# A product that nothing reads behind each hop of a triangular solve

## The chip, the cores and the metric

The kernel runs on one core of a Trainium2 chip. Its time is the device time of one execution in microseconds (us); lower is better. Three executions of the kernel before took 1478.14, 1480.52 and 1487.08 us, median 1480.52.

## The reference

The model has four layers, each with a residual sum behind a layer norm: a selective scan, an attention with a mixture of experts, a causal layer, and the attention with experts again. The change lies in the causal layer, for 4 batches of 512 positions, 16 heads of 8:

```python
probs = jax.nn.softmax(logits + causal_mask, axis=-1)
L = jnp.eye(s, dtype=probs.dtype) - jnp.tril(probs, -1)
rhs = jnp.diagonal(probs, axis1=-2, axis2=-1)[..., None] * v
A = jax.scipy.linalg.solve_triangular(L, rhs, lower=True)
```

So every position is the weighted sum of all earlier solved positions and its own value, and the solve is serial along the positions.

## The kernel before

The function `delta_phase` computes this layer. It works on 16 tiles of 128 positions, four to a batch; the loop index is `n`, and `t = n % 4` is the tile's place in its batch. Each engine has a program written out by hand in the same order: a loop over `n` from -6 to 15, and inside it 14 numbered places, the hooks `h` (0 to 13). At a hook `beside(n, h)` puts in work for later tiles: row maxima of tile `n + 4` or `n + 3` (L2772 and L2775 on TensorE, read by VectorE at L2559), scores of tile `n + 3` (L2790, L2793, L2802, read by ScalarE at L2400 and L2405), the sums of tile `n + 2`, and at hooks 9 to 12 the products `mt` of tile `n + 1` (L2839, copied by ScalarE at L2412). Between these stands the solve of tile `n` itself.

The solve of a tile: for `t` above 0 the earlier tiles' contribution (L2887), turned (L2906); then a product with the inverses of the 16x16 diagonal blocks (L2915, at hook 2); then seven hops (L2928), at hooks 3, 5, 7, 9, 10, 11 and 12. Before each hop VectorE transposes 32 columns of the step's PSUM bank into `a_hop` (L2700), and behind the last one ScalarE copies the solved tile to `aT` (L2452). A hop is 16 small fp32 products, each with 16 or 32 rows and 32 columns of the array, four of them side by side on the diagonal of the array. The last of them raises the semaphore `at_ps` for VectorE or ScalarE. Then TensorE goes on with the next hook.

Transfers are queued on SyncE: the sums of a tile go to DRAM and back (`z_scr`), GpSimd inverts the blocks, and the inverses go out and back (`x_scr`) before `mt` can be computed. The keys and queries of the next batch (`k_scr`, `q_scr`) are loaded once the last scores of the batch before have been computed.

PSUM has eight banks of 512 fp32 columns per partition: two for the steps, `TURN` (number 2) for two transposes a tile, two that ScalarE reads and three that VectorE reads. `TURN` is written at the start of a tile (`turned`, L2938, and `turn_right_side`, L2906) and read by ScalarE (L2456) and VectorE (L2691) before the product of L2915.

`mask_diag4` is a bf16 table of 128x512 and `ident_b` the bf16 identity; `score` uses the same pair at L2790 to start a bank.

Of the kernel before, what the change touches and what calls it, by code (L numbers as in the profile page):

```python
# [1918 lines left out]
def delta_phase(core, nc):  # L1919

    x_sb, w = core.x, core.w
    q_scr, k_scr, m_scr = core.q_scr, core.k_scr, core.md_scr
    e_scr, z_scr, x_scr = core.e_scr, core.z_scr, core.x_scr
    with ExitStack() as ctx:
# [3 lines left out]
        ps = ctx.enter_context(nc.psum_tensor("d_ps", [P, 8, 512], F32))  # L1928

        STEP, TURN, TO_ACT, TO_DVE = (0, 1), 2, (3, 4), (5, 6, 7)  # L1930
# [252 lines left out]
        def all_mt(n):  # L2183
            return in_act("mt", n, len(MT_HOOKS) - 1)
# [8 lines left out]
        with nc.Block() as block:  # L2193
# [525 lines left out]
            def _(pe):  # L2719
# [5 lines left out]
                def dve_free(kind, n, i=0):  # L2725
                    if dve_place[kind, n, i] >= 3:
                        pe.wait_ge(s["dve_out"], dve_place[kind, n, i] - 2)
                    return dve_bank(kind, n, i)
# [115 lines left out]
                def beside(n, h):  # L2844
                    if n >= 1 and h == 0:
                        output(n - 1)
                    m = later_tile_at(turned_sums_at, n, h)
                    if m is not None:
                        turn_sums(m)
                    if starts_in(n, 4) is not None and h in (6, 7):  # L2850
                        own_scores(starts_in(n, 4), h - 6)
                    m = maxima_done(n, h)
                    if m is not None:
                        turn_maxima(m)
                    for i in scores_in(n, h):
                        score(n + 3, i)
                    for m, hd in maxima_in(n, h):
                        for_maximum(m, hd)
                    if in_program(n + 1) and h in MT_HOOKS:
                        multiplied(n + 1, MT_HOOKS.index(h))  # L2860
                    m = later_tile_at(sums_at, n, h)
                    if m is not None:
                        sums(m)
                    m = tile_at(column_at, n, h)
                    if m is not None:
                        turn_column(m)
                    if goes_on(n, LEAD) is not None and h == 12:
                        turn_in(goes_on(n, LEAD))
                    if batch_at(values_at, n, h) is not None:
                        project_values(batch_at(values_at, n, h))  # L2870
                    if begins_early(n + 1) and h == 13:
                        first_tiles(n + 1)
                    if goes_on(n, 5) is not None and h in (0, 1):
                        project(goes_on(n, 5), h)

                def output(n):
                    pe.wait_ge(s["at_sb"], n + 1)
                    nc.tensor.matmul(dve_free("output", n)[:, 0:P], aT[:, n % 2, :], w["d_wd"], start=True, stop=True).then_inc(
                        s["dve_ps"], 1)
# [17 lines left out]
                def from_earlier(n):  # L2897
                    t = n % TPB
                    pe.wait_ge(s["an_sb"], turned_tiles(n - 1))
                    if n >= 2:  # L2900
                        pe.wait_ge(s["at_sb"], n - 1)
                    earlier_tiles(n, range(t - 1, t)).then_inc(s["g_ps"], 1)

                def turn_right_side(n):
                    pe.wait_ge(s["gT_sb"], later_tiles(n))
                    nc.tensor.transpose(ps[:, TURN, 0:P], gT[:, :], core.ident[:, :]).then_inc(s["gn_ps"], 1)  # L2906

                def inverse(n):
                    pe.wait_ge(s["gn_sb"], n + 1)
                    if n >= 2:  # L2910
                        pe.wait_ge(s["at_sb"], n - 1)
                    for g in range(GROUPS):
                        for q in range(GROUP):
                            hd = g * GROUP + q
                            last = nc.tensor.matmul(ps[q * SPAN:(q + 1) * SPAN, STEP[n % 2], 0:P], of_head(g_pad[:, :], hd),  # L2915
                                                    xT[:, n % 2, hd, :], start=(g == 0), stop=(g == GROUPS - 1))
                    last.then_inc(s["at_ps"], 1)

                def hop(n, k):
                    if k == 1:  # L2920
                        pe.wait_ge(s["act_out"], all_mt(n))
                    pe.wait_ge(s["hop_in"], HOPS * n + k)
                    r = (k - 1) // 2
                    rows, cols = (BLK, slice(BLK, SPAN)) if k % 2 else (SPAN, slice(SPAN, P - r * SPAN))
                    for g in range(GROUPS):
                        for q in range(GROUP):
                            own = slice(q * SPAN, q * SPAN + rows)
                            last = nc.tensor.matmul(  # L2928
                                ps[q * SPAN:(q + 1) * SPAN, STEP[n % 2], r * SPAN + cols.start:r * SPAN + cols.stop],
                                a_hop[own, g * SPAN:(g + 1) * SPAN],  # L2930
                                mT[own, n % 2, g, SPAN_AT[r] + cols.start:SPAN_AT[r] + cols.stop],
                                start=False, stop=(g == GROUPS - 1), skip_group_check=True)
                    last.then_inc(s["at_ps"], 1)

                def turned(n):
                    pe.wait_ge(s["at_sb"], n + 1)
                    pe.wait_ge(s["gn_sb"], n + 1)
                    nc.tensor.transpose(ps[:, TURN, 0:P], aT[:, n % 2, :], core.ident[:, :]).then_inc(s["an_ps"], 1)  # L2938

                for n in range(-LEAD, TILES_N):  # L2940
                    later = n >= 0 and n % TPB
                    if n == 0:
                        pe.wait_ge(s["set"], 4)
                        pe.wait_ge(s["zero_set"], 2)
                    if later:
                        turned(n - 1)
                    for h in range(HOOKS):
                        beside(n, h)
                        if later and h == 0:
                            from_earlier(n)  # L2950
                        if later and h == 1:
                            turn_right_side(n)
                        if n >= 0 and h == 2:
                            inverse(n)
                        if n >= 0 and h in HOP_AFTER:
                            hop(n, HOP_AFTER[h])
                output(TILES_N - 1)

# [86 lines left out]
```

## Time and profile before

| | |
|---|---|
| median of 3 runs | 1480.52 us |
| the profiled execution, its own time | 1479.21 us |
| its span, first to last instruction | 1477.3 us |
| TensorE (PE) busy | 1156.5 us, 78% |
| VectorE (DVE) busy | 999.9 us, 68% |
| ScalarE (ACT) busy | 684.1 us |
| GpSimd (POOL) busy | 631.6 us |
| granted clock of TensorE, mean | 0.868 |

### The profile page before, as it was taken

Reading aid. Unit: us, or ns where it says so; the run is one execution under the profiler, and the core shown is the slowest. Engines: PE = TensorE matmul, PEld = TensorE weight load, DVE = VectorE, ACT = ScalarE, POOL = GpSimd, SP = SyncE. Lnnn points to the kernel's source line nnn. Section 1 sums busy time; section 2 is a strip of 40 time slices with the busy share of each in tenths; the row PEclk is TensorE's granted clock in tenths of the full one; section 3 lists DMA queues with packets and bytes.
Section 4 is the critical chain, followed back from the end, with each engine's and each line's share of the span. In section 5 each row is a group of like instructions: output and inputs, shape, how many; then the busy total and the mean of one; then the engine's idle time right before and its main releaser. Section 6 shows DMA issues by size and latency. Waiting matters only on the chain. (4 is left out here: it accounts for less than half of the span.)

```text
span 1477.3 us, 32913 instructions
## 1 busy us (share of the span) xinstructions
PE 1156.5 (78%) x12859; PEld 628.3 (43%) x12890; DVE 999.9 (68%) x2098; ACT 684.1 (46%) x1380; POOL 631.6 (43%) x838
## 2 busy tenths in 40 slices
PE   6746776869999998636868877968866699999976
PEld 2212232323333327623546655645655333333276
DVE  6699999978898965446635635625621688989653
ACT  3833334406667674512603513432341066676754
POOL 2279979852435124413334324422432524351244
PEclk9878879879999998856868968977997599999998
DMA  5388834033133121262241141141120331331213
GB/s 168 140 278 311 300 142 146 32 82 88 27 97 93 44 79 49 65 130 34 37 87 22 30 103 19 23 105 27 20 53 11 68 88 35 88 94 42 83 48 91
DMA packets 137744, 128.49 MB, mean 87 GB/s; under 512 B 92007, under 2 KB 123559, under 8 KB 132202
## 3 DMA queue, kind: packets, MB, share of 16 engines
q1 hardware_dynamic: 129536, 118.50, 29.1%
q0 software_dynamic: 2496, 5.13, 1.1%
q10 hardware_dynamic: 5558, 2.76, 0.9%
q8 instruction: 102, 1.67, 0.5%
q14 instruction: 52, 0.43, 0.1%
HBM read 105.55 MB, written 38.62 MB: 98 GB/s over the span
## 5 line engine op out<-in xcount | busy, mean ns | idle before, releaser
L1391 DVE TENSOR_REDUCE f_row_min<-f_ps 128x1 f32<-128x512 f32 x512 | 323.8, 676 | 55.1 <-PE f_ps L1718 54.8
L1281 ACT ACTIVATE f_e<-f_ps 128x512 f32<-128x512 f32 x512 | 283.0, 602 | 125.0 <-PE f_ps L1738 123.2
L1718 PE MATMUL f_ps<-f_operands 72*128 72x512 bf16 x512 | 204.6, 409 | 27.7 <-DMA f_operands<-k_scr 16.2
L1738 PE MATMUL f_ps<-f_operands 75*128 75x512 bf16 x512 | 189.5, 380 | 2.6 <-ACT f_e L1281 2.6
L788 PE MATMUL m_ps<-m_shared,sb_ident 128*128 128x512 f32 x256 | 136.1, 681 | 58.2 <-DVE m_shared L628 58.1
L361 POOL TENSOR_TENSOR m_drive<-m_du,m_ring 128x1024 f32<-128x1024 f32 x64 | 149.6, 2351 | 56.2 <-DVE m_ps L620 37.7
L2559 DVE TENSOR_REDUCE d_row_min<-d_ps 128x1 f32<-128x384 f32 (+3 forms) x176 | 104.6, 630 | 74.3 <-PE d_ps L2775 73.6
L493 ACT ACTIVATE m_ps<-m_delta,m_A 128x511 f32<-128x511 f32 x128 | 83.0, 681 | 131.6 <-DVE m_ps L620 109.0
L1749 PE MATMUL f_ps<-f_e,f_v_op 128*32 128x512 f32 x1024 | 136.4, 604 | 2.1 <-ACT f_e L1281 1.4
L1718 PEld LDWEIGHTS f_ps<-f_operands 72*128 72x128 bf16 x512 | 51.2, 100 | 180.6 <-DVE f_row_min L1391 129.2
L788 PEld LDWEIGHTS m_ps<-m_shared,sb_ident 128*128 128x128 f32 x256 | 52.6, 216 | 143.7 <-DVE m_shared L628 86.9
L620 DVE TENSOR_TENSOR_SCAN m_ps<-m_ps,m_drive 128x1024 f32<-128x1024 f32 x44 | 101.1, 2297 | 4.9
L2212 POOL TENSOR_TENSOR d_xT_blk<-d_e_blk,d_zi_blk 128x256 f32<-128x256 f32 x16 | 13.3, 832 | 202.9 <-DVE d_zi_blk L2620 202.9
L2772 PE MATMUL d_ps<-d_k_op,d_q_op 96*128 96x128 bf16 (+3 forms) x256 | 71.4, 360 | 36.1 <-DMA d_k_op<-k_scr 23.0
L2412 ACT COPY d_mT<-d_ps 128x320 f32<-128x320 f32 x64 | 27.3, 426 | 131.0 <-PE d_ps L2839 130.2
L2839 PE MATMUL d_ps<-d_xT,d_e_nat 128*32 128x128 f32 (+3 forms) x2048 | 64.1, 282 | 24.6 <-DMA d_xT<-x_scr 21.9
L2928 PE MATMUL d_ps<-d_mT,d_a_hop 16*32 16x16 f32 (+3 forms) x3584 | 71.3, 216 | 8.0 <-DVE d_a_hop L2700 7.0
L2223 POOL TENSOR_TENSOR d_xT_blk<-d_xT_blk,d_prod 128x14 f32<-128x14 f32 (+6 forms) x224 | 63.8, 285 | 17.5
L2700 DVE STREAM_TRANSPOSE d_a_hop<-d_ps 128x32 f32<-128x32 f32 x112 | 23.7, 211 | 70.0 <-PE d_ps L2928 57.5
L1168 POOL DMA_INDIRECT y_scr<-f_operands x46 | 53.7, 1168 | 38.8 <-DVE f_operands L1607 36.9
L2839 PEld LDWEIGHTS d_ps<-d_xT,d_e_nat 128*32 128x32 f32 x2048 | 55.5, 135 | 34.8 <-DMA d_xT<-x_scr 23.8
L2218 POOL TENSOR_TENSOR d_prod<-d_xT_blk 128x14 f32<-128x14 f32 (+6 forms) x224 | 62.1, 277 | 17.5
(295 smaller groups left out, 2177.2 us busy)
## 6 DMA issues: line engine op xcount, KB each, us to landing
m_ring<-bc_scr SPq DMA_DIRECT2D x32, 1024.0 KB, 5.4
f_rows_scr<-blank SPq DMA_DIRECT2D x2, 8707.5 KB, 31.1
f_wall<-f_wall SPq DMA_DIRECT2D x16, 578.0 KB
f_operands<-q_scr SPq DMA_DIRECT2D x32, 288.0 KB
f_operands<-k_scr SPq DMA_DIRECT2D x96, 96.0 KB
d_q_op<-q_scr SPq DMA_DIRECT2D x6, 576.0 KB
d_k_op<-k_scr SPq DMA_DIRECT2D x18, 192.0 KB
f_operands<-f_rows_scr SPq DMA_DIRECT2D x46, 64.5 KB, 1.8
```

Of the source, the lines that this page charges most:

```text
L361: nc.gpsimd.tensor_tensor(drive[:, step % AHEAD, :].rearrange("p (a s) -> p a s", a=HALVES), du[:, :, tokens(b)], b_row(step).unsqueeze(1) ...
L493: last = nc.scalar.activation(ps[:, at + 1:at + S], delta[:, k, b * S + 1:(b + 1) * S], ACT.Exp, scale=A[:, k, n:n + 1])
L620: nc.vector.tensor_tensor_scan(h, bank(DECAY + HALVES * (step % 2), HALVES), drive[:, step % AHEAD, :], 0.0, ALU.mult, ALU.add).then_inc(s ...
L788: last = nc.tensor.matmul(bank(Y + k), core.ident[:, :], hC[:, k * S:(k + 1) * S], start=False, stop=last_of_batch)
L1281: nc.scalar.activation(e_sb[:, n % 3, hh, :], ps[:, SCORE[(b * UNITS + u) % SCORE_BANKS], :], ACT.Exp, scale=SCALE).then_inc(s["e_out"], 1)
L1391: nc.vector.tensor_reduce(row_min[:, b % 2, u // TPB, u % TPB:u % TPB + 1], ps[:, MAXQ[(b * UNITS + u) % MAX_BANKS], :], AX.X, ALU.max, ne ...
L1718: nc.tensor.matmul(ps[:, MAXQ[n % MAX_BANKS], :], q_op(b, QK)[:, hd, t * P:(t + 1) * P], k_op(b, QK)[:, hd, :], start=True, stop=True).the ...
L1738: nc.tensor.matmul(ps[:, SCORE[n % SCORE_BANKS], :], k_op(b, QKS)[:, hd, t * P:(t + 1) * P], q_op(b, QKS)[:, hd, :], start=True, stop=True ...
L1749: last = nc.tensor.matmul(ps[hh * HEAD_COLS:(hh + 1) * HEAD_COLS, O_BANK, :], v_of(b, t, g * GROUP + hh), e_sb[:, n % 3, hh, :], start=(t ...
L2559: nc.vector.tensor_reduce(row_min[:, n % 2, g * heads:(g + 1) * heads], dve_bank("maximum", n, g)[:, 0:heads * cols].rearrange("p (h c) -> ...
L2772: nc.tensor.matmul(bank[:, hh * cols:(hh + 1) * cols], q_op[0:SHIFT_AT, hd, rows_of(t)], k_op[0:SHIFT_AT, hd, 0:cols], start=(hh == 0), st ...
L2839: last = nc.tensor.matmul(bank[q * SPAN:(q + 1) * SPAN, SPAN_AT[r]:SPAN_AT[r] + P - first], e_nat[:, n % 3, hd, first:first + SPAN], xT[:, ...
```

## The change

Behind each of the seven hops of each tile TensorE computes one more product: the identity, over all 128 rows and columns of the array, with the 512 columns of `mask_diag4`, bf16, into the bank `TURN`. It raises no semaphore and waits for none. Nothing reads the result; the next product that uses the bank starts it anew.

```diff
@@ -2932,6 +2932,9 @@
                                 start=False, stop=(g == GROUPS - 1), skip_group_check=True)
                     last.then_inc(s["at_ps"], 1)
 
+                def keep_busy():
+                    nc.tensor.matmul(ps[:, TURN, :], w["ident_b"], w["mask_diag4"], start=True, stop=True)
+
                 def turned(n):
                     pe.wait_ge(s["at_sb"], n + 1)
                     pe.wait_ge(s["gn_sb"], n + 1)
@@ -2954,6 +2957,7 @@
                             inverse(n)
                         if n >= 0 and h in HOP_AFTER:
                             hop(n, HOP_AFTER[h])
+                            keep_busy()
                 output(TILES_N - 1)
```

The order of the other instructions stays as it is on every engine; only PE's program grows, by 16 x 7 = 112 products. The difference of PE's program at the first two hops of tile 0 (L2928 is the hop, L2936 the added product, L2802 scores and L2755 sums for later tiles):

```order
 L2828 MATMUL d_ps<-sb_ident,d_z_col 16x128
 L2928 MATMUL d_ps<-d_mT,d_a_hop 32x16 x16
+L2936 MATMUL d_ps<-sb_mask_diag,sb_ident_b 128x512
 L2802 MATMUL d_ps<-d_q_op,d_k_op 128x128 x12
 L2928 MATMUL d_ps<-d_mT,d_a_hop 32x96 x16
+L2936 MATMUL d_ps<-sb_mask_diag,sb_ident_b 128x512
 L2755 MATMUL d_ps<-sb_head_sum,d_swap 128x16 x2
 L2802 MATMUL d_ps<-d_q_op,d_k_op 128x128 x6
```

The added product stands between the hop and the work for later tiles; the hop's semaphore is raised ahead of it.

## Rows read from the trace of the kernel before

**Rows 1.** The page: span, busy time of engines, granted clock in 40 slices.
```profile
span 1477.3 us, 32913 instructions
...
PE 1156.5 (78%) x12859; PEld 628.3 (43%) x12890; DVE 999.9 (68%) x2098; ACT 684.1 (46%) x1380; POOL 631.6 (43%) x838
...
PEclk9878879879999998856868968977997599999998
```

**Rows 2.** Windows by tile: us; PE, PEld, DVE, ACT, POOL busy; PEclk; DMA share; GB/s.
```profile
723.70:756.00 32.30, 23.05 (x594) 17.49 (x592) 10.48 (x25) 13.64 (x33) 11.33 (x33) 0.86 0.51 110
756.00:788.10 32.10, 24.17 (x518) 17.74 (x524) 16.26 (x43) 6.03 (x15) 9.64 (x31) 0.66 0.20 28
788.10:818.60 30.50, 25.70 (x607) 18.87 (x608) 17.31 (x53) 10.22 (x22) 12.00 (x33) 0.89 0.20 33
818.60:841.20 22.60, 19.42 (x528) 14.39 (x529) 17.95 (x45) 9.13 (x20) 11.14 (x30) 0.92 0.12 13
841.20:871.70 30.50, 24.27 (x594) 18.98 (x592) 10.26 (x26) 13.58 (x33) 10.27 (x32) 0.80 0.50 113
871.70:904.20 32.50, 23.52 (x518) 17.44 (x524) 16.27 (x44) 6.03 (x15) 9.63 (x31) 0.71 0.20 31
904.20:937.20 33.00, 27.59 (x607) 20.56 (x608) 17.15 (x54) 10.32 (x22) 12.00 (x33) 0.84 0.20 32
937.20:957.90 20.70, 18.55 (x535) 13.68 (x536) 17.83 (x45) 9.16 (x21) 9.56 (x27) 1.00 0.07 9
1023.70:1054.80 31.10, 24.89 (x599) 18.18 (x601) 16.52 (x53) 10.41 (x22) 10.79 (x32) 0.89 0.18 30
1099.70:1151.20 51.50, 31.88 (x1161) 26.27 (x1160) 5.82 (x26) 5.47 (x16) 9.66 (x31) 0.76 0.09 14
723.70:1151.20 427.50, 327.32 (x8461) 246.97 (x8486) 193.37 (x531) 136.09 (x319) 147.45 (x441) 0.82 0.24 46
```

**Rows 3.** What PE waited for in 723.7:1151.2: total us, times, longest.
```profile
PE d_ps L2772 <- DMA d_k_op<-k_scr: 23.0, 6, 6.3
PE d_ps L2839 <- DMA d_xT<-x_scr: 21.9, 9, 7.3
PE d_ps L2780 <- DVE d_row_min L2559: 20.5, 9, 4.3
PE d_ps L2928 <- DVE d_a_hop L2700: 7.0, 19, 0.6
```

**Rows 4.** The tile d_ps: the hop's products, min/median/max ns, forms.
```profile
L2928 PE MATMUL d_ps<-d_mT,d_a_hop x3584: 171/209/365, 725.1 to 1150.6; 16*32 16x16 f32 x116, 32*32 32x96 f32 x28, 32*32 32x64 f32 x28, 32*32 32x32 f32 x28
```

**Rows 5.** Timeline of PE, one 512-column product at the higher clock level.
```profile
787.99 0.39 PE L2790 MATMUL d_ps<-sb_mask_diag,sb_ident_b 128*128 128x512 bf16 x1
788.21 0.27 PE L2793 MATMUL d_ps<-d_k_op,d_q_op 128*128 128x128 bf16 x2
```

**Rows 6.** Timeline of PE, one 512-column product at the lower clock level.
```profile
752.18 0.63 PE L2775 MATMUL d_ps<-sb_mask_up,sb_ident_b 128*128 128x512 bf16 x1
752.60 0.42 PE L2906 MATMUL d_ps<-sb_ident,d_gT 128*128 128x128 f32 x1
```

**Rows 7.** Timeline of PE: four idle gaps behind hops, with what ended them.
```profile
742.26 0.33 PE L2938 MATMUL d_ps<-sb_ident,d_aT 128*128 128x128 f32 x1 [0.40 <-ACT d_aT L2452]
...
798.00 1.03 PE L2839 MATMUL d_ps<-d_xT,d_e_nat 128*32 128x128 f32 x32 [2.58 <-DMA d_xT<-x_scr]
...
987.85 0.61 PE L2772 MATMUL d_ps<-d_k_op,d_q_op 96*128 96x128 bf16 x4 [6.26 <-DMA d_k_op<-k_scr]
...
1007.62 0.38 PE L2780 MATMUL d_ps<-sb_ident,d_row_min 128*16 128x128 f32 x1 [2.90 <-DVE d_row_min L2559]
```

**Rows 8.** Timeline of PE and DVE, one round of the last tile.
```profile
1148.28 0.62 PE L2928 MATMUL d_ps<-d_mT,d_a_hop 16*32 16x16 f32 x32 [0.34 <-DVE d_a_hop L2700]
1148.97 0.22 DVE L2700 STREAM_TRANSPOSE d_a_hop<-d_ps 128x32 f32<-128x32 f32 x1 [0.74 <-PE d_ps L2928]
```

**Rows 9.** Window inside the tile that starts at 756.0, no long gap.
```profile
759.00:768.90 9.90, 9.88 (x132) 6.48 (x132) 7.21 (x18) 0.47 (x2) 0.00 (x0) 0.50 0.25 42
```

## The prediction, made before the changed kernel ran

> **What bounds the kernel now.** I read the page first: PE is busy for 1156.5 of 1477.3 us, and its granted clock is high nearly everywhere except at the start and in the middle [rows 1]. The change touches only the solves, so I then read windows by tile. The sixteen solves take 427.5 us, with PE busy for 327.3 and DVE for 193.4, at a clock of 0.82 [rows 2]: PE works at its lower level for 2 x 0.18 x 427.5 = 154 us. Third, the waits: the 100 us in which PE is idle there are in good part waits for transfers, 23.0 us for keys and 21.9 us for block inverses, and 20.5 us for DVE's row maxima; the hops themselves waited only 7.0 us for DVE's transposes [rows 3]. So PE sets the pace between a few waits that others set, and both a longer PE program and a faster PE clock show only in part.
>
> **The added work, gross.** The nearest row is the same product with the same operands, L2790: from its start to the next product's start 788.21 - 787.99 = 0.22 us at the higher level [rows 5]. At the lower level a product of the same size took 752.60 - 752.18 = 0.42 us [rows 6]. With 36% of the time at the lower level the mean is 0.64 x 0.22 + 0.36 x 0.42 = 0.29 us, and 112 of them are 32.7 us. That is the upper end of the cost, with nothing hidden. The trace has no product of this kind between two packed groups; I take the price as it is, since the hop's small products (171 to 365 ns each, four side by side) [rows 4] give way to full-array products in the same program already.
>
> **What of it is hidden.** A product behind a hop costs nothing if PE would have waited before the next thing that matters, and the wait's end doesn't depend on it. I go by the tile's place t in its batch; seven products each, 1.5 us at the higher level, up to 2.9 at the lower.
> - t = 0. Hops 1 to 3 stand ahead of the wait for inverses (2.58 us in one case [rows 7]), whose chain started a tile earlier; I count them hidden for most of it. Hops 4 to 7 stand ahead of the wait for the next batch's keys (6.26 us [rows 7]), whose loads were released by earlier scores. The seventh also falls into the 0.40 us in which PE waits for ScalarE's copy [rows 7]. Left over: about 0.6 us a tile, 4 tiles, 2.4 us.
> - t = 1. Hops 1 to 3 lie in the row maxima that DVE limits, with a wait of 2.90 us at their end [rows 7] against 3 x 0.42 = 1.3 us added. Hops 4 to 7 stand before small waits for ScalarE. Left: 0.6 us, 4 tiles, 2.4 us.
> - t = 2. Hops 1 to 4 are ahead of waits for inverses and maxima, 5 to 7 are exposed. Left: 0.8 us, 4 tiles, 3.2 us.
> - t = 3. PE is densest here, 18.55 of 20.70 us [rows 2]; small waits for maxima and copies take up most. Left: 0.4 us, 3 tiles, 1.2 us.
> - The last tile has nothing beside the hops. From the end of the hop (1148.28 + 0.62 = 1148.90) DVE's transpose starts at 1148.97 and takes 0.22 us, and PE idles 0.34 us before the next hop [rows 8]. The product streams through most of that gap. I count 0.1 us in all.
>
> The sum is 9.3 us. The transfers are not delayed much: what releases them is later by the same few tenths. If these covers go (a transfer released late by the products, a faster load), up to the full 32.7 us shows; the lower end is 0.
>
> **What it may give back: the clock.** Tiles of the same kind at different clocks tell what the lower level costs. For t = 3: 22.60 us at 0.92 against 20.70 us at 1.00, so 2 x 0.08 x 22.6 = 3.6 us at the lower level cost 1.9 us. For t = 2: 33.00 us at 0.84 (10.6 us low) against 31.10 at 0.89 (6.8 us low), 1.9 us for 3.8 us more [rows 2]; the third, 30.50 us at 0.89, lies beside the second. So with t = 2 and 3 about 0.55 us is lost for each us at the lower level. With t = 0 and 1 there is no such relation: 32.30 us at 0.86 against 30.50 at 0.80, and 32.10 at 0.66 against 32.50 at 0.71 [rows 2]; their waits for transfers take up the difference.
>
> How much low time goes cannot be read from a row; it is bounded by none and by all. In rows 9 PE is busy for 9.88 of 9.90 us and the clock stays at 0.50 throughout [rows 9]. So being busy was not enough there; what runs in it are products over 96 rows and hops that use 16 or 32 rows and columns each [rows 4]. The added product uses the whole array, which most of the beside work does not, and the clock may rise for it. The Trainium skill, page "TensorE: Matmul & The Clock Gate", section "What's actually happening", says that the gate is set by how busy PE has been recently and that activity releases it; taken as busy time it would have the clock high in this window, which the trace contradicts, and it would give the added products nothing to do there.
>
> I take half of the low time for t = 2 and 3 in the first three batches. There it is 6.7 + 3.6 + 10.6 + 0 + 6.8 = 27.7 us over the five rows, so 13.9 x 0.55 = 7.6 us. From 1099.7 on, where PE is only 62% busy, 0.48 x 51.5 = 24.7 us are low [rows 2]; a third of that at 0.4 gives 3.3 us. The rest of the low time, some 102 us with t = 0 and 1, I count at nothing, since waits stand behind it. Together 11 us. The bounds: nothing, and all of it, 0.55 x 27.7 + 0.5 x 24.7 + 0.15 x 102 = 43 us.
>
> **The sum** is 1479.2 + 9.3 - 11 = 1477.5 us for an execution like the profiled one, which lies 1.3 us under the median of the three. Against the median: **1479 us**. Under 1% (15 us, so 1465.7 to 1495.3) counts as no change that can be told.
>
> **The rivals.**
> - *The clock doesn't move.* By the skill's rule read as busy time. The mechanism here: where the clock is low, PE waits around the hop, or is busy already as in rows 9. Then only the 9.3 us remain: 1490 us. For it, rows 9; against it, that the product uses four to eight times as much of the array as four small products of a hop side by side [rows 4]. 15%, no change.
> - *The products lie on the path (slower).* Place: between a hop and the beside work at hooks 3 to 12. ScalarE and DVE get scores, maxima and `mt` later by 0.22 to 0.42 us each, and SP sends sums and inverses later, so that the waits for transfers move instead of shrinking. Two thirds unhidden are 22 us: 1502 us with the clock as it is; all of it 1513. It decides from 15 / 32.7 = 46% unhidden with no clock returned. For it: PE is the busiest engine in every tile [rows 2]. Against: some 65 us of waits for transfers and maxima [rows 3] stand behind the hops. 18%.
> - *The clock stays high through most of it (faster).* Two thirds of the bound on the gain, 29 us, less 9: 1460 us. It decides when over 24 us are given back. For it: seven products a tile are spread over the tile, also where the clock falls. Against: in the long waits, 6.26 us and the like [rows 7], no hop stands. 20%.
> - *It doesn't do what it says*: `TURN` would have to be in use or the product to bring a wait. Program order shows neither. 2%, 1480 us.
>
> The forecast itself has 45%.
>
> **Range and chances.** Within 1%: 45 + 15 + 2 = 62%; faster 20%; slower 18%. The range takes in half of either side case: from 1462 to 1499 us.
>
> **What would show it.** In the changed trace, the line of the added product: 112 of them, starts 0.22 us or 0.42 us ahead of the next product. The clock over the solves above 0.82, with the tiles of t = 3 at 1.00 near 21 us, and those of t = 2 above 0.89. The wait of PE for DVE's row maxima and for the inverses shorter by about a third. The tiles with t = 0 and 1 within 1 us of before. The forecast is wrong if the clock over the solves stays at 0.82 and the waits don't shrink (slower), or if it goes over 0.92 (faster).

## The result and the profile after

In 20 executions each, the changed kernel took 1487.25 us (median; 1481.16 to 1495.94) and the kernel before 1481.29 us (1476.72 to 1489.74). The ratio is 1.0036, with a 95% interval of 1.0019 to 1.0054: 5.3 us slower (2.8 to 8.0). It lies within the 1% that the forecast counted as no change and in its range, but the forecast of 1479 us was on the other side of 1, and the loss is clear of noise. One execution of either kernel is a few us off its median, so a cost of 5 us is read from the timed ratios; the profiles, one execution each (1486.8 us here), tell where clock and waits moved.

The page of the changed kernel, the lines that answer to [rows 1]:

```profile
span 1485.0 us, 33058 instructions
...
PE 1155.3 (78%) x12892; PEld 632.8 (43%) x13002; DVE 999.6 (67%) x2098; ACT 683.7 (46%) x1380; POOL 630.9 (42%) x838
...
PEclk9879889869999998857969977978987699999988
```

The windows by tile, in the columns of [rows 2] and at the same places of the program (tile by tile from the step's first transpose, then the tail and all solves):

```profile
722.40:755.80 33.40, 23.33 (x595) 18.32 (x601) 9.97 (x26) 13.57 (x33) 11.56 (x34) 0.86 0.50 106
755.80:788.80 33.00, 24.14 (x523) 17.72 (x531) 16.16 (x44) 6.02 (x15) 9.57 (x31) 0.73 0.19 28
788.80:820.40 31.60, 26.09 (x609) 19.53 (x615) 17.66 (x54) 10.21 (x22) 11.97 (x33) 0.89 0.21 33
820.40:842.10 21.70, 18.99 (x534) 14.41 (x541) 17.63 (x44) 9.11 (x20) 10.02 (x29) 1.00 0.10 12
842.10:874.80 32.70, 22.69 (x591) 17.92 (x594) 10.39 (x27) 13.57 (x33) 11.54 (x34) 0.86 0.48 108
874.80:907.40 32.60, 23.42 (x523) 17.38 (x531) 16.05 (x43) 6.02 (x15) 9.57 (x31) 0.77 0.19 28
907.40:939.80 32.40, 27.04 (x609) 20.37 (x616) 17.64 (x53) 10.22 (x22) 11.97 (x33) 0.84 0.21 32
939.80:961.30 21.50, 19.04 (x537) 14.42 (x544) 17.86 (x45) 9.21 (x21) 9.84 (x28) 1.00 0.10 12
1027.40:1057.90 30.50, 26.09 (x601) 19.54 (x607) 16.67 (x53) 10.39 (x22) 10.73 (x32) 0.83 0.19 31
1106.00:1159.20 53.20, 32.18 (x1167) 26.70 (x1182) 5.94 (x26) 5.46 (x16) 9.57 (x31) 0.81 0.08 13
722.40:1159.20 436.80, 327.76 (x8495) 251.50 (x8601) 193.28 (x531) 135.86 (x319) 147.43 (x442) 0.85 0.24 45
```

The solves take 436.8 us where they took 427.5 [rows 2]. The clock over them rose from 0.82 to 0.85, so 2 x 0.15 x 436.8 = 131 us are low instead of 154. The tiles show where. The tile with t = 3 that was at 0.92 is at 1.00 and takes 21.70 instead of 22.60 us; the one that was at 1.00 before takes 21.50 instead of 20.70, so seven products, 1.5 us gross, cost 0.8 us there. The forecast had 0.4. The tiles with t = 2, where the forecast looked for the return, stand at 0.89, 0.84 and 0.83, no better than 0.89, 0.84 and 0.89 before [rows 2]. Those with t = 1 rose, from 0.66 and 0.71 to 0.73 and 0.77, and did not get shorter (33.00 and 32.60 us). Those with t = 0 take 33.40 and 32.70 us, 1.1 and 2.2 us longer. The tail went from 0.76 to 0.81, 24.7 to 20.2 us low, and takes 53.20 us instead of 51.50.

What PE waited for in the solves, as [rows 3] (total us, times, longest):

```profile
PE d_ps L2839 <- DMA d_xT<-x_scr: 25.2, 9, 7.2
PE d_ps L2772 <- DMA d_k_op<-k_scr: 23.4, 6, 5.3
PE d_ps L2780 <- DVE d_row_min L2559: 17.3, 12, 3.7
```

Two of these waits were to shrink by a third. The one for the row maxima shrank from 20.5 to 17.3 us, the one for the inverses grew from 21.9 to 25.2 [rows 3]. The trace has every weight load of the new products, but not every product (kind, count, min/median/max ns, first and last start):

```profile
L2936 PEld LDWEIGHTS d_ps<-sb_mask_diag,sb_ident_b x112: 94/96/103, 724.3 to 1158.7; 128*128 128x128 bf16 x112
L2936 PE MATMUL d_ps<-sb_mask_diag,sb_ident_b x18: 389/390/607, 726.9 to 1157.9; 128*128 128x512 bf16 x18
```

So 94 products are missing in its PE busy time, and the idle time of this profile is overstated; the profile of the narrow products below has all 112. The price is as forecast, as one product at the higher level shows in the timeline, 822.46 - 822.23 = 0.23 us:

```profile
822.23 0.39 PE L2936 MATMUL d_ps<-sb_mask_diag,sb_ident_b 128*128 128x512 bf16 x1
822.46 0.61 PE L2802 MATMUL d_ps<-d_q_op,d_k_op 128*128 128x128 bf16 x8
```

### The profile page after: what moved, and what is told of

Same layout as the page of the kernel before. It is cut to its first block and busy times, and to the rows that moved or that the text cites. A ratio compares the mean times of both kernels' runs of the same rounds, so it can differ in the third digit from the quotient of the medians.

```text
span 1485.0 us, 33058 instructions
## 1 busy us (share of the span) xinstructions
PE 1155.3 (78%) x12892; PEld 632.8 (43%) x13002; DVE 999.6 (67%) x2098; ACT 683.7 (46%) x1380; POOL 630.9 (42%) x838
## 5 line engine op out<-in xcount | busy, mean ns | idle before, releaser
L2212 POOL TENSOR_TENSOR d_xT_blk<-d_e_blk,d_zi_blk 128x256 f32<-128x256 f32 x16 | 13.3, 833 | 206.6 <-DVE d_zi_blk L2620 206.6
L2772 PE MATMUL d_ps<-d_k_op,d_q_op 96*128 96x128 bf16 (+3 forms) x256 | 68.9, 351 | 37.1 <-DMA d_k_op<-k_scr 23.4
L2839 PE MATMUL d_ps<-d_xT,d_e_nat 128*32 128x96 f32 (+3 forms) x2048 | 63.7, 279 | 36.1 <-DMA d_xT<-x_scr 25.2
L2928 PE MATMUL d_ps<-d_mT,d_a_hop 16*32 16x16 f32 (+3 forms) x3584 | 69.1, 213 | 3.5 <-DVE d_a_hop L2700 2.8
```

The costliest lines, as they stand in the source:

```text
L2839: last = nc.tensor.matmul(bank[q * SPAN:(q + 1) * SPAN, SPAN_AT[r]:SPAN_AT[r] + P - first], e_nat[:, n % 3, hd, first:first + SPAN], xT[:, ...
```

## The experiments

All ratios are against the kernel before on the same chip, with 95% intervals. Each kernel ran 12 times, e11_full_rows 11 and e10_narrow_double 6 times. Two terms were open, the hidden share of the products and the return of the clock.

**e1_narrow** takes the array away and leaves the stream:

```diff
-                    nc.tensor.matmul(ps[:, TURN, :], w["ident_b"], w["mask_diag4"], start=True, stop=True)
+                    nc.tensor.matmul(ps[0:32, TURN, :], w["ident_b"][0:32, 0:32], w["mask_diag4"][0:32, :], start=True, stop=True)
```

> The added product keeps its 512 columns and its place, but uses 32 rows and 32 columns of the array instead of 128 and 128, so PE streams as long as in the changed kernel. Theory A (the clock did give back about 10 us as forecast, and the hidden part was overrated, so that some 15 us of the products lie on the path): without the return the time is the kernel before plus 14 to 17 us, ratio about 1.010, and the clock over the solves is back at about 0.82. Theory B (the products cost the 6 us that are seen, and the clock returns nothing): the same as the changed kernel, ratio about 1.004. The low time in the solves (152 us before, 133 us changed) tells too: A wants it at 150 or more.

Measured: 1490.21 us, ratio 1.0068 (1.0041 to 1.0096), 10 us slower. Its window over the solves and its waits:

```profile
721.90:1159.40 437.50, 359.85 (x8573) 254.26 (x8598) 193.24 (x530) 136.07 (x319) 147.93 (x442) 0.81 0.24 45
```

```profile
PE d_ps L2839 <- DMA d_xT<-x_scr: 19.2, 9, 5.0
PE d_ps L2780 <- DVE d_row_min L2559: 16.8, 9, 3.8
PE d_ps L2772 <- DMA d_k_op<-k_scr: 15.6, 5, 4.9
```

The clock is at 0.81. At 0.38 x 0.42 + 0.62 x 0.22 = 0.30 us a product, 112 are 33 us gross. PE is busy for 359.85 us, 32.5 us more than before, while the solves grew by 437.5 - 427.5 = 10.0 us; so some 23 us went into idle time, which fell from 100.2 to 77.6 us. The three waits show 13.8 us of it: 15.6, 19.2 and 16.8 against 23.0, 21.9 and 20.5 [rows 3]. So a stream without the return costs 10 us, between the two theories (14 to 17, and 6). That is an upper bound for the cost term, forecast as 9.3, because the narrow products also leave the clock somewhat lower than it was before, as the clocks of all executions show below.

**e10_narrow_double** and **e3_double** put two narrow and two whole products behind each hop. The edit of e3 (e10 has the narrow line twice):

```diff
                     nc.tensor.matmul(ps[:, TURN, :], w["ident_b"], w["mask_diag4"], start=True, stop=True)
+                    nc.tensor.matmul(ps[:, TURN, :], w["ident_b"], w["mask_diag4"], start=True, stop=True)
```

> Two such products behind each hop instead of one. Theory A: the cost doubles to 30 us or a little more, since the gaps are used up, and the clock returns somewhat more than with one, 12 to 16 us: the kernel before plus 16 to 20 us, ratio about 1.012. Theory B: two times 6 us and what no longer fits in the gaps, 14 to 20 us, ratio 1.010 to 1.013. If the clock stays high almost throughout (over 0.92 in the solves), the time may come out under that of one product: ratio under 1.004.

> Two products behind each hop, each over 32 rows and 32 columns of the array, 512 columns long: the stream of e3_double without its use of the array. Theory A (the cost on the path is some 10 us for one product a hop, and the clock gave back 4 us of it with one whole-array product and much more with two): 20 to 24 us slower than before, ratio 1.014 to 1.016, against 1.0042 for e3_double. Theory B (the clock returns nothing, and a second product fits into gaps that the first has opened): the same as e3_double, 1.004.

Measured: the whole ones 1488.11 us, ratio 1.0042 (1.0018 to 1.0067); the narrow ones 1507.99 us, ratio 1.0198 (1.0171 to 1.0225). The same streams at the same places are 29 us slower or 6 us slower than the kernel before, by what part of the array they use. The whole ones came near the case that was set apart in their expectation (a clock over 0.92, a ratio under 1.004), the narrow ones lie above the 1.014 to 1.016 of theory A. The windows over the solves, the narrow ones first:

```profile
721.10:1171.60 450.50, 386.99 (x8685) 258.03 (x8710) 192.33 (x531) 136.52 (x319) 148.66 (x446) 0.81 0.23 43
```

```profile
719.20:1152.10 432.90, 338.50 (x8603) 243.89 (x8710) 193.00 (x531) 135.71 (x319) 148.43 (x446) 0.92 0.24 45
```

The clock is at 0.81 with the narrow products and at 0.92 with the whole ones. So, between two kernels with equal streams, the clock is worth about 23 us, and which of the two has the higher clock goes with the use of the array and not with busy time: PE is busy for 86% of the solves in the narrow kernel, and for 78% in the other, 83% if the 97 products that its trace lacks are added at 0.22 us. Part of the 23 us is the products' own price. In the narrow kernel, two of them start 0.22 us apart at the higher level and 0.43 at the lower:

```profile
725.52 0.37 PE L2936 MATMUL d_ps<-sb_mask_diag,sb_ident_b 32*32 32x512 bf16 x1
725.74 0.37 PE L2937 MATMUL d_ps<-sb_mask_diag,sb_ident_b 32*32 32x512 bf16 x1
...
734.90 0.63 PE L2936 MATMUL d_ps<-sb_mask_diag,sb_ident_b 32*32 32x512 bf16 x1
735.33 0.63 PE L2937 MATMUL d_ps<-sb_mask_diag,sb_ident_b 32*32 32x512 bf16 x1
```

With 38% and 16% of the solves low, 224 products are 224 x (0.38 - 0.16) x 0.2 = 10 us cheaper in e3_double.

**e11_full_rows** has all rows and 32 columns of the array:

```diff
-                    nc.tensor.matmul(ps[:, TURN, :], w["ident_b"], w["mask_diag4"], start=True, stop=True)
+                    nc.tensor.matmul(ps[0:32, TURN, :], w["ident_b"][:, 0:32], w["mask_diag4"], start=True, stop=True)
```

> One product behind each hop over all 128 rows but only 32 columns of the array, 512 long: PE streams as long as in the changed kernel, with a quarter of the array. Theory A (the return needs the whole array): like e1_narrow, 9 to 11 us slower than before, ratio 1.006 to 1.007. If what counts is that all rows are fed, it is like the changed kernel, 1.0036. Theory B (no return at all, e1_narrow's difference is chance): 1.0036 too; e10_narrow_double then tells these two apart.

Measured: 1487.17 us, ratio 1.0047 (1.0027 to 1.0067). The time tells nothing apart; for single products the intervals of whole, narrow and this one touch or overlap. The clock does. Over the solves it is at 0.86, with all 112 products in the trace, as high as in the changed kernel (0.85) and not as with the narrow ones (0.81):

```profile
724.10:1158.20 434.10, 348.67 (x8573) 249.21 (x8598) 194.28 (x531) 135.76 (x319) 147.89 (x441) 0.86 0.24 45
```

**The clock of every execution.** A profile is one execution, but every execution has its mean granted clock c over the whole program. With the span T, 2 x (1 - c) x T of it are at the lower level. Means over all executions:

| kernel | clock | kernel before | low time against before, us | time against before, by the ratio, us |
|---|---|---|---|---|
| changed | 0.880 | 0.872 to 0.874 | -17 to -23 | +5.3 |
| e1_narrow | 0.867 | 0.872 | +18 | +10.1 |
| e11_full_rows | 0.882 | 0.874 | -22 | +7.0 |
| e3_double | 0.896 | 0.872 | -70 | +6.2 |
| e10_narrow_double | 0.857 | 0.874 | +57 | +29.3 |
| e2_short | 0.871 | 0.872 | +3 | -1.2 |
| e4_late_tiles | 0.874 | 0.872 | -6 | +4.4 |
| e5_early_tiles | 0.879 | 0.873 | -16 | +5.6 |
| e7_t2_double | 0.878 | 0.873 | -13 | +3.1 |
| e6_fill_keys | 0.880 | 0.873 | -22 | -2.7 |
| e9_fill_both | 0.891 | 0.874 | -51 | -3.1 |
| e12_fill_more | 0.896 | 0.873 | -66 | -3.4 |

(For the changed kernel the clocks of its own runs of the kernel before are not on record; the range is that of the four chips of the experiments. The low times are good to about 10 us, that of e10 to about 20.)

Three things follow. First, 32 columns over all 128 rows raised the clock as much as the whole array did, and 32 columns over 32 rows lowered it: the single executions of e11_full_rows lie at 0.877 to 0.886, those of e1_narrow at 0.857 to 0.876. The rows made the difference, the other 96 columns none that shows. Second, the narrow products are no clean measure of the cost, since they add low time; the return against the kernel before is smaller than what separates whole from narrow. Third, the price of low time: between e10_narrow_double and e3_double 127 us of it go with 23 us, 0.18 us for each, with what the products themselves cost more at the lower level included. Between executions of one and the same kernel it is alike: in 109 of the kernel before, each us more at the lower level went with 0.20 us more time (correlation 0.66). That is a correlation, not an experiment, but the forecast had taken 0.5.

**e2_short** leaves whole-array products of 16 columns:

```diff
-                    nc.tensor.matmul(ps[:, TURN, :], w["ident_b"], w["mask_diag4"], start=True, stop=True)
+                    nc.tensor.matmul(ps[:, TURN, 0:16], w["ident_b"], w["mask_diag4"][:, 0:16], start=True, stop=True)
```

> The added product uses the whole array but streams 16 columns instead of 512: the weight load and the switch from small packed products to a whole-array product stay, the stream goes. Theory A and B both price the stream, so this should cost 112 x about 0.03 us = 3 us gross, 1 to 2 us on the path: ratio 1.000 to 1.001. Theory C (the switch itself costs, by breaking up the packed products): most of the 6 us stay, ratio 1.003 to 1.004.

Measured: 1481.18 us, ratio 0.9992 (0.9971 to 1.0013). Loading the identity and switching between packed and whole-array products costs nothing that can be measured (at most 2 us by the interval), and the clock stays where it was; the stream is the cost.

**Where the products stand.** e4_late_tiles keeps them for t = 2 and 3, e5_early_tiles for t = 0 and 1, e7_t2_double two of them for t = 2 only, e8_last_hop one only behind the seventh hop. The edit of e4; the others have `n % TPB < 2`, `n % TPB == 2` and `HOP_AFTER[h] == HOPS` as condition:

```diff
                             hop(n, HOP_AFTER[h])
+                            if n % TPB >= 2:
-                            keep_busy()
+                                keep_busy()
```

> The products stand only in the tiles with t = 2 and 3 (56 of 112), where the forecast placed the whole return of the clock. Theory A with the return where it was forecast: cost and return about cancel, ratio 0.999 to 1.001, and the loss of the changed kernel lies in the tiles with t = 0 and 1. Theory B: half of the loss, ratio 1.002. If it is 1.004 the loss lies in these dense tiles.

> The products stand only in the tiles with t = 0 and 1 (56 of 112), the other half of e4_late_tiles. If the losses of the two halves add up to that of the changed kernel (ratio 1.0036), this one has about 1.001, since e4 has 1.003. Theory A (a cost of about 9 to 10 us that the narrow product showed, less a return of the clock of about 4): these tiles hide the products behind the waits for keys and inverses as the forecast said, and the cost lies in t = 2 and 3. Theory D (the waits for transfers move with the products and hide nothing): ratio 1.003 here as well, and the halves don't add up because the clock's return in e4 is lost.

> Two products behind each hop, but only in the four tiles with t = 2 (56 products). In the profile of e3_double these tiles had 10 us at the lower level instead of 34, and took 112.3 instead of 117.2 us. Theory A (low time costs about half of itself in these tiles, as the forecast took it): 3 to 5 us faster than before, ratio 0.997 to 0.998. Theory B (the clock returns next to nothing): 3 to 6 us slower, ratio 1.002 to 1.004.

> A product only behind the seventh hop of each tile (16 products), where PE waits 0.35 to 0.40 us for ScalarE's copy of the solved tile, except ahead of the tiles with t = 2 and 3. Hidden as forecast: gross 4 us, about 1 us on the path, ratio 1.000 to 1.001. If that gap doesn't hide it, ratio 1.002 to 1.003.

Measured: e4 1.003 (1.0006 to 1.0053), e5 1.0038 (1.0021 to 1.0054), e7 1.0021 (0.9996 to 1.0046), e8 1.0001 (0.9979 to 1.0023). The halves cost 4.4 and 5.6 us, together 10 us, as much as the narrow products in all places, while the whole costs 5.3: it looks as if half of the products return next to nothing, though the intervals leave room for additive halves, and the low times do add up (6 and 16 us against 17 to 23). The tiles with t = 0 and 1 hide the products no better than the others; e5 leaves out the 1.001 of theory A. e7 missed: with two products the low time of the t = 2 tiles should have been worth more than the products, and it isn't, so the 0.55 us for each low us that I read from pairs of tiles doesn't arrive at the end. Its profile, which is its fastest execution (1476.86 us), has the three tiles with t = 2 of the first three batches:

```profile
787.10:816.20 29.10, 26.78 (x623) 18.17 (x622) 17.65 (x53) 10.23 (x22) 11.98 (x33) 1.00 0.21 34
903.20:933.20 30.00, 28.08 (x623) 18.97 (x623) 18.12 (x53) 10.22 (x22) 11.98 (x33) 0.94 0.21 33
1017.50:1048.30 30.80, 27.11 (x615) 17.92 (x614) 16.60 (x52) 10.40 (x22) 10.76 (x32) 0.94 0.19 32
```

Together they take 89.9 us, with 42 products in them, instead of 94.6 [rows 2], and are low for 7 us instead of 24. So in these tiles the return did come, about as the forecast priced it. 0.55 x 17 us given back, less 0.8 us for each of six sets of seven products, is 4.6 us. But the tiles with t = 0 of the same batches, which have no added product, take 101.7 us instead of 97.0 (36.2, 33.3 and 32.2 against 32.3, 30.5 and 34.2), and all solves 426.9 instead of 427.5. The gain is gone in the next tiles; with one execution each, whether by the transfers that they wait for or by chance stays open. Behind the seventh hop no cost of the products shows, as forecast, though the interval reaches to 3.4 us.

**Filling waits instead.** e6_fill_keys has no product behind a hop, but 12 and 8 ahead of the two waits for the keys of the next batch; e9_fill_both has also 4, 14 and 20 ahead of the wait for the inverses; e12_fill_more has 20 and 12, and 7, 24 and 32. In `for_maximum` and in `multiplied` (e9):

```diff
                     if n >= TPB and t == 0 and g * heads in (0, NH // 2):
+                        for _ in range(12 if g == 0 else 8):
+                            nc.tensor.matmul(ps[:, TURN, :], w["ident_b"], w["mask_diag4"], start=True, stop=True)
...
+                    if i == 0 and n >= 1:
+                        for _ in range({14: 14, 15: 20}.get(n, 4 if n % 2 else 0)):
+                            nc.tensor.matmul(ps[:, TURN, :], w["ident_b"], w["mask_diag4"], start=True, stop=True)
```

> No product behind a hop. Instead 12 and 8 such products ahead of PE's two waits for the next batch's keys (three batches, 60 products), where PE idles 2.3 to 6.3 us, so the products should be free (60 x 0.22 = 13 us, all inside 23.0 us of waits). Theory A: the clock enters the tiles with t = 1 at its higher level, their low time falls from 72 us to 30 to 45 us. If low time costs nothing there, as the forecast had it, ratio 0.999 to 1.001; if it costs 0.3 us for each us there, 10 us are gained, ratio 0.993 to 0.996. If the waits aren't free, ratio over 1.003.

> No product behind a hop. The 60 products ahead of the waits for keys as in e6_fill_keys, and 62 more ahead of PE's wait for the block inverses at hook 9: 4 in each of the tiles 0, 2, 4 to 12 where it waits 0.5 to 2.6 us, 14 and 20 in tiles 13 and 14, where it waits 4.9 and 7.3 us. If filling idle time is free and the clock enters the dense ends of the t = 2 tiles and the tail at its higher level, as I now hold: 3 us faster than e6_fill_keys, 5 to 6 us faster than before, ratio 0.996. If waits shorter than the filling make it late: ratio 0.999 to 1.001.

> As e9_fill_both with longer fillings: 20 and 12 products ahead of the two waits for keys (96 in all), 7 in each of seven tiles and 24 and 32 in tiles 13 and 14 ahead of the wait for inverses (105 in all). In e9_fill_both PE still waited 10.5 and 15.3 us at these two places. If low time is worth something where it is left, and filling stays free: 1 to 3 us faster than e9_fill_both, ratio 0.996 to 0.997. If, as I now hold, the low time that goes lies behind waits and row maxima and is worth next to nothing, while the longer fillings overrun some of the waits: ratio 0.998 to 1.001.

Measured: e6 1477.56 us, ratio 0.9982 (0.9961 to 1.0003); e9 1476.84 us, 0.9979 (0.9961 to 0.9996); e12 1479.91 us, 0.9977 (0.9956 to 0.9999). All three lie between what their two theories gave. For e6 and e9 no cost shows, and the kernels with 122 and 201 of them are about 3 us faster than the kernel before, with intervals that only just stay under 1; the kernel of this case is slower than both. The windows over the solves of e6, e9 and e12:

```profile
726.50:1148.40 421.90, 333.10 (x8549) 243.65 (x8547) 192.97 (x531) 136.09 (x319) 147.68 (x444) 0.87 0.25 46
```

```profile
720.80:1148.00 427.20, 336.48 (x8568) 244.79 (x8608) 193.73 (x531) 136.32 (x319) 150.70 (x447) 0.89 0.25 46
```

```profile
724.70:1155.20 430.50, 347.63 (x8647) 246.42 (x8687) 191.80 (x531) 135.99 (x319) 147.53 (x442) 0.91 0.25 45
```

The clock goes to 0.87, 0.89 and 0.91, so in these profiles 110, 94 and 77 us are low instead of 154 (over all executions the fall is smaller, 22, 51 and 66 us), and the gain stays at 3 us: the low time that went was worth next to nothing, or the fillings cost what it was worth. The latter isn't ruled out for e12, where PE waits for the inverses 0.4 us in all instead of 21.9, so that its longer fillings ran past some transfers. In return PE's wait for VectorE's row maxima grew from 20.5 us [rows 3] to 21.9, 27.6 and 30.9 us. The timeline of e6 in a tile with t = 1 shows how (in its numbering L2769 is the filling, L2774 and L2782 are L2772 and L2780 of before):

```profile
991.86 2.71 PE L2769 MATMUL d_ps<-sb_mask_diag,sb_ident_b 128*128 128x512 bf16 x8
994.40 0.39 PE L2774 MATMUL d_ps<-d_k_op,d_q_op 96*128 96x128 bf16 x4
...
996.39 0.28 PE L2782 MATMUL d_ps<-sb_ident,d_row_min 128*16 128x128 f32 x1 [0.46 <-DVE d_row_min L2559]
...
1006.59 0.38 PE L2782 MATMUL d_ps<-sb_ident,d_row_min 128*16 128x128 f32 x1 [4.63 <-DVE d_row_min L2559]
```

From 994.40 on PE is at the higher level (its products are 0.39 us long, not 0.61 to 0.64), is done with its part of the maxima sooner, and then waits 4.63 us for VectorE's last one, where it waited 2.90 us before [rows 7]. That product starts at 1006.59, 12.2 us behind the end of the wait for keys; before it started at 1007.62, 13.3 us behind it, with the clock at the lower level all the while. About 12 us at the higher level brought 1.1 us:

```profile
994.34 0.61 PE L2772 MATMUL d_ps<-d_k_op,d_q_op 96*128 96x128 bf16 x4 [2.31 <-DMA d_k_op<-k_scr]
```

## Why the prediction was wrong

- *Price of a product*, 0.22 and 0.42 us: right; 0.23 us in the changed kernel, 0.22 and 0.43 in e10_narrow_double. The doubt about packed groups is answered by e2_short: no cost of switching.
- *What is on the path*, 9.3 of 32.7 us: near in size, as far as the runs tell. Without any return it would be the 5.3 us measured, and e1_narrow gives at most 10 us (6 to 14) of 33. Its split over tiles isn't confirmed: e5_early_tiles costs at least as much as e4_late_tiles, where the forecast had 4.8 and 4.4 us with about 11 us of return in the latter. For t = 3 the tiles that were at 1.00 before and after show 0.8 us where the forecast had 0.4.
- *"I take half of the low time for t = 2 and 3"*, with a third for the tail, priced at 0.55 and 0.4: this is the step that failed, the return of 11 us. That the clock can give time back is shown by the doubled pair. Its size is at most 10.1 - 5.3 = 4.8 us for one product a hop (0 to 10 by the two intervals), since the narrow products add low time of their own. The amount of low time that went was as assumed (154 to 131 us in the profiles, 17 to 23 us over all executions, against 13.9 + 8.2), but not its place: the five rows of t = 2 and 3 hold 7.0 + 0 + 10.4 + 0 + 10.4 = 27.8 us of low time, against 27.7 before. It went with t = 1, from 21.8 to 17.8 and from 18.9 to 15.0 us in the two tiles shown, where the forecast rightly counted it at nothing, and in the tail, 4.5 us, which came out longer all the same. At the 0.18 to 0.20 us for each low us of all executions, some 20 us give 4 us: an estimate that agrees with 4.8.
- *The 0.55 us for each low us*: borne out inside the tiles with t = 2 of e7_t2_double, not at the end of the program. A tile that is shorter in the profile is not yet a shorter kernel; where e7's gain went stays open.
- *The reading of rows 9*, that products over 96 rows and small hops ran there: incomplete. Ten products of L2775 over the whole array ran there too, 4.23 us of PE's busy time, two of them 512 columns long, and the clock stayed at 0.50. So whole-array products don't bring the clock up everywhere, and the reason given for a rise was weaker than it looked:

```profile
759.32 0.63 PE L2775 MATMUL d_ps<-sb_mask_up,sb_ident_b 128*128 128x512 bf16 x1
```

- *Net*: -1.7 us forecast, +5.3 measured; 9.3 - 11 against at most 10.1 - 4.8. That it ended within 1% is luck, and no merit of the working: the cost and the return are both small against the 15 us.
- *The rival that the clock doesn't move* (1490 us) came near in time, but not in its mechanism: the clock over the solves rose from 0.82 to 0.85. The Trainium skill, page "TensorE: Matmul & The Clock Gate", section "What's actually happening", says that the gate is set by how busy PE has been recently. Read as busy time, this disagrees with the pair: PE is busy for 86% of the solves at 0.81 in e10_narrow_double, and for no more in e3_double at 0.92.
- *The rival on the path* (1502 us): its place was right for at most 10 us, not for 22.
- *The rival that the clock stays high* (faster) needs two products a hop, and then they cost more than the clock returns: e3_double, 0.92 and yet 1.0042.
- *What would show it*: waits for maxima and inverses a third shorter was wrong, they went from 20.5 to 17.3 and from 21.9 to 25.2 us; t = 2 above 0.89 was wrong, and so was t = 0 within 1 us (1.1 and 2.2 us longer); a clock above 0.82, t = 1 within 1 us and t = 3 at 1.00 near 21 us were right.

## What to carry to other kernels

Before one adds work to hold TensorE's clock, take the same stream with a corner of the array and with all its rows; the pair shows what the clock is worth, and one kernel alone does not. The corner gives only an upper bound on the cost, because it can lower the clock: look at the granted clock of all executions, not at one profile. Low time is worth something only where PE's own stream ends last; ahead of a wait for a transfer or for VectorE it was worth next to nothing here, however much of it there was. Such work belongs ahead of a wait that is longer than it, where it did no harm, rather than behind each step of a serial chain; even there it brought only 3 us of 1480.

## What the runs showed of the hardware

- With equal streams at equal places, two products a hop over 32 rows and columns left the clock over the solves at 0.81 and two over the whole array raised it to 0.92; that was 23 us of 1508.
- With one product a hop, 128 rows and 32 columns raised the mean clock of the program from 0.874 to 0.882, 128 rows and columns to 0.880, while 32 rows and columns lowered it from 0.872 to 0.867.
- A whole-array weight load and a 16-column product between packed groups, 112 times, cost nothing measurable (0.9992) and left the clock alone (0.871 against 0.872).
- Matmul records of the whole-array products directly behind a hop were missing in bulk in three profiles (18 of 112 present in the changed kernel, 15 of 112 in e3_double, 10 of 56 in e4_late_tiles) and complete in others (56 of 56 in e5_early_tiles, 28 of 28 in e7_t2_double); their weight loads and the second product of each pair were always there. What decides it is not known.
